# A recurrence of 64 chunks: corrections in two sets, new orders on four engines, TensorE's loop closed at another place

## The reference, cut to what matters

```python
def step(carry, inp):
    W1c, b1c = carry
    xq, xk, xv, et = inp
    Z1 = xk @ W1c + b1c
    grad = _ln_l2_bwd(Z1, xv - xk, g, bb)
    Attn1 = jnp.tril(xq @ xk.swapaxes(-1, -2))
    b1_bar = b1c - jnp.tril(et) @ grad
    Z1_bar = xq @ W1c - et * Attn1 @ grad + b1_bar
    last_eta = et[..., -1, :, None]
    W1n = W1c - (last_eta * xk).swapaxes(-1, -2) @ grad
    b1n = b1c - (last_eta * grad).sum(-2, keepdims=True)
    return ((W1n, b1n), xq + _ln(Z1_bar, g, bb, EPS_IN))
```

## Time and profile before

| | us |
|---|---|
| median of 3 runs | 583.49 (583.01 to 584.29) |
| the profiled execution | 581.06 |
| its span, first to last instruction | 579.2 |
| busy: PE, DVE, ACT, POOL | 483.9, 432.1, 346.2, 327.8 |
| mean granted clock of TensorE, share of full speed | 0.959 |

### The profile page before, as it was taken

The page is one execution under the profiler, slowest core; times in us unless marked ns, Lnnn a source line. Parts: engine busy times, 40 slices in busy tenths (PEclk is TensorE's granted clock), DMA queues, the critical chain, the costliest instruction groups (busy, mean ns, idle before and its releaser), DMA issues.

```text
span 579.2 us, 30352 instructions
## 1 busy us (share of the span) xinstructions
PE 483.9 (84%) x12556; PEld 313.8 (54%) x12556; DVE 432.1 (75%) x1526; ACT 346.2 (60%) x1166; POOL 327.8 (57%) x590
## 2 busy tenths in 40 slices
PE   0699889898558789888888888888887699998996
PEld 0344334443346577777777676666675244456563
DVE  4757788888746789888888888888885667676652
ACT  2344334322246788888888889988885487553321
POOL 1276888787734466666666655565763667330112
PEclk9999989899858999999999999999997899998998
DMA  8310111111101011111111000011010500000123
GB/s 338 123 24 14 37 37 36 38 36 36 39 9 32 22 37 28 33 32 33 33 28 37 1 1 1 19 36 37 19 37 4 171 1 2 1 2 1 74 75 145
DMA packets 15136, 24.74 MB, mean 43 GB/s; under 512 B 4228, under 2 KB 4968, under 8 KB 15080
## 3 DMA queue, kind: packets, MB, share of 16 engines
q1 hardware_dynamic: 15080, 24.10, 13.8%
HBM read 11.50 MB, written 4.19 MB: 27 GB/s over the span
## 4 chain that ended last, share of the span: by engine, by line
PE 25%; DVE 24%; ACT 12%; issue 8%; POOL 2%; POOLq 0%; ACTq 0%
PE PS L1167 6%; PE PS L924 4%; PE PS L1255 3%; PE PS L906 3%; ACT work L1556 3%; PE PS L361 2%; DVE work L1341 2%; DVE work L1336 2%; DVE work L1322 2%; DVE work L1300 2%; DVE work L1319 2%; DVE PS L1338 2%; DVE PS L1323 2%; DVE PS L1302 2%; DVE PS L1325 2%
## 5 line engine op out<-in xcount | busy, mean ns | idle before, releaser
L1167 PE MATMUL PS<-work 32*32 32x32 f32 x4064 | 59.6, 194 | 37.9 <-DVE work L1341 21.0
L1167 PEld LDWEIGHTS PS<-work 32*32 32x32 f32 x4064 | 53.8, 108 | 43.4 <-issue 43.1
L1411 POOL TENSOR_TENSOR work<-work,mask 128x256 f32<-128x256 f32 x64 | 46.8, 731 | 35.7 <-ACT work L1531 35.7
L512 PE MATMUL PS<-X,work 128*128 128x512 f32 x128 | 63.2, 641 | 0.3 <-ACT X L435 0.3
L1423 POOL TENSOR_TENSOR work<-work,lrh 128x4 f32<-128x4 f32 x64 | 12.9, 201 | 75.6 <-DVE work L1314 70.1
L1300 DVE TENSOR_REDUCE work<-work 128x4 f32<-128x128 f32 x64 | 18.3, 286 | 49.2 <-ACT work L1556 49.2
L663 POOL TENSOR_TENSOR work<-work 128x512 f32<-128x512 f32 x32 | 43.8, 1370 | 7.1 <-DVE work L582 7.1
L1152 PEld LDWEIGHTS PS<-work 64*32 64x32 f32 x2048 | 32.9, 110 | 24.9 <-issue 23.6
L1152 PE MATMUL PS<-work 64*32 64x64 f32 x2048 | 43.6, 225 | 2.9 <-issue 2.0
L1194 PE MATMUL PS<-cst 128*128 128x256 f32 x126 | 45.1, 440 | 0.0
L1179 PE MATMUL PS<-work 32*64 32x32 f32 x2016 | 43.0, 222 | 2.2 <-issue 2.2
(11 more groups left out here) (162 smaller groups left out, 1344.5 us busy)
## 6 DMA issues: line engine op xcount, KB each, us to landing
X<-in_x SPq DMA_DIRECT2D x4, 1024.0 KB, 8.2
TK<-KP SPq DMA_DIRECT2D x64, 64.0 KB, 1.9
X<-QP SPq DMA_DIRECT2D x64, 64.0 KB, 2.0
TK<-in_x SPq DMA_DIRECT2D x16, 256.0 KB, 3.0
out<-TK SPq DMA_DIRECT2D x16, 256.0 KB, 2.4
work<-in_rope SPq DMA_DIRECT2D x2, 512.0 KB, 9.1
cst<-in_consts SPq DMA_DIRECT2D x1, 289.0 KB, 5.0
work<-in_wk SPq DMA_DIRECT2D x1, 256.0 KB, 11.2
```

The source lines that it names most:

```text
L512: mm = nc.tensor.matmul(PS[:, 2 + m, :], lhs(j), xt(i, j), start=(j == 0), stop=(j == J - 1))
L1167: mm = nc.tensor.matmul(PS[HD * a:HD * a + HD, bank, b * width:b * width + HD], AM[p][HD * a:HD * a + HD, b, part, :, :].rearrange("p e t ...
L1411: nc.gpsimd.tensor_tensor(AM[p].rearrange("p b s e t -> p (b s) e t"), S1[p].unsqueeze(2).broadcast_to([P, 2 * B, E, CS]), mask2.rearrange ...
```

## The change

On VectorE the correction's two terms become operands of their own: WX moves from PSUM to SBUF, YC is made before cc1, one reduction and one product change places, and `out_var` comes ahead of GL. TensorE runs the correction twice, with YC as soon as that is there and with WX when that is (`front`), then waits for GL for the update and the attention. `front` holds corrections, update, attention and, where asked, the filler; `back` holds the next base and the query base. Chunks 0 to 1 and the front of 2 are written out, then come two loops, of 3 and of 12 trips, which begin with a back and end with a front, and then chunk 62's back and chunk 63. The filler is in the fronts 1 and 2 and in three of four fronts of the first loop.

VectorE's out_turn writes straight into TT; the tile ZT, ScalarE's `out_store` and the waits between them go, also those behind the last chunk (not shown: there `out_store` five times and four waits of VectorE). On GpSimd out_norm and queries come first; masks and blocks come last, behind a new wait for GL, in exchanged order. On ScalarE qt2 goes behind products.

```diff
...
@@ -754,11 +754,11 @@
         S1 = [carve(B * 2, CS) for _ in range(2)]
         AM = [carve(B, 2, E, CS) for _ in range(2)]
         Bs = [carve(B, HD) for _ in range(2)]
-        TS, SQ, YL, YC = (carve(B, HD) for _ in range(4))
+        TS, SQ, YL, YC, WX = (carve(B, HD) for _ in range(5))
         YY = carve(2, B, HD)
         GL = [carve(B, HD) for _ in range(2)]
         ZQ = [carve(B, HD) for _ in range(3)]
-        SQQ, ZN, ZT = (carve(B, HD) for _ in range(3))
+        SQQ, ZN = (carve(B, HD) for _ in range(2))
         ss, sz, ssq, sd1 = (carve(B) for _ in range(4))
         vq = [carve(2 * B) for _ in range(2)]
         var1, sdq = [v[:, 0:B] for v in vq], [v[:, B:2 * B] for v in vq]
...
@@ -1111,16 +1111,7 @@
 
                 return c >= n if isinstance(c, int) else n <= 2
 
-            def run_chunks(eng, body):
-
-                for c in range(2):
-                    body(c, c % 2)
-                with nc.Fori(0, NC // 4 - 1, engines=(mybir.EngineType.PE,), hint_back_edge=True) as four:
-                    for k in range(4):
-                        body(four * 4 + (2 + k), k % 2)
-                for c in range(NC - 2, NC):
-                    body(c, c % 2)
-
+            FILLED = 3
             GAIN_AT, PRE_AT = NC // 2 + 8, NC - 8
             QROWS_AT, PIECES, INPUTS_AT = 3, 2 * J * E, NC // 2 + 14
             is_last = lambda c: isinstance(c, int) and c == NC - 1
@@ -1160,14 +1151,14 @@
                         Bs[1 - p if past(n, 1) else 0], start=False, stop=False, skip_group_check=True
                         ).then_inc(q["base"], 1)
 
-                def grads(width, bank, p, part):
+                def grads(width, bank, p, part, rows):
 
                     for b in range(B):
                         for a in range(4):
                             mm = nc.tensor.matmul(PS[HD * a:HD * a + HD, bank, b * width:b * width + HD],
                                                   AM[p][HD * a:HD * a + HD, b, part, :, :].rearrange(
                                                       "p e t -> p (e t)"),
-                                                  GL[p][HD * a:HD * a + HD, b, :],
+                                                  rows[HD * a:HD * a + HD, b, :],
                                                   start=False, stop=True, skip_group_check=True)
                     return mm
 
...
@@ -1194,36 +1185,12 @@
                     nc.tensor.matmul(PS[:, QB[p], 256:512], ident, ccol("spread", 0, 256), start=True, stop=True,
                                      skip_group_check=True)
 
-                def body(c, p):
-
-                    o = 1 - p
-                    done, now, nxt = value(pe, c), value(pe, c + 1), value(pe, c + 2)
-                    before = value(pe, c - 1) if past(c, 2) else None
-                    if past(c, 1):
-                        pe.wait_ge(q["init"], 1)
-                        pe.wait_ge(q["gl"], done)
-                        pe.wait_ge(q["am"], done)
-                        pe.wait_ge(q["s1"], now)
-                        grads(ZW, ZB[p], o, 1).then_inc(q["corr"], 1)
-                        pe.wait_ge(q["init"], 1)
-                        pe.wait_ge(q["khx"], done)
-                        pe.wait_ge(q["bcopy"], done)
-                        update(o)
-                        grads(HD, QB[o], o, 0).then_inc(q["attn"], 1)
-                        if past(c, 2):
-                            pe.wait_ge(q["zq"], before)
-                        filler(p)
-                    else:
-                        base(0, 0, 1, 1)
-                    if not is_last(c):
-                        base(c + 1, o, nxt, now)
-                    else:
-                        pe_mean(pe, 0, True)
+                def query_base(ready, p, drained):
                     pe.wait_ge(q["init"], 1)
-                    pe.wait_ge(q["qt2"], now)
-                    pe.wait_ge(q["wcopy"], now)
-                    if past(c, 2):
-                        pe.wait_ge(q["zq"], before)
+                    pe.wait_ge(q["qt2"], ready)
+                    pe.wait_ge(q["wcopy"], ready)
+                    if drained is not None:
+                        pe.wait_ge(q["zq"], drained)
                     for b in range(B):
                         for k in range(J):
                             for a2 in range(2):
@@ -1231,14 +1198,59 @@
                                 mm = nc.tensor.matmul(
                                     PS[HD * a:HD * a + HD, QB[p], b * HD:b * HD + HD],
                                     QT2[p][r:r + 64, k * B + b, :, :].rearrange("p e t -> p (e t)"),
-                                    R[o][r:r + 64, k, b, 0:HD], start=(b == 0), stop=False,
+                                    R[1 - p][r:r + 64, k, b, 0:HD], start=(b == 0), stop=False,
                                     skip_group_check=True)
                     mm.then_inc(q["qbase"], 1)
 
-                run_chunks(pe, body)
+                def front(p, before, done, now, fill):
+
+                    o = 1 - p
+                    pe.wait_ge(q["init"], 1)
+                    pe.wait_ge(q["yc"], done)
+                    pe.wait_ge(q["am"], done)
+                    pe.wait_ge(q["s1"], now)
+                    grads(ZW, ZB[p], o, 1, YC)
+                    pe.wait_ge(q["init"], 1)
+                    pe.wait_ge(q["w"], done)
+                    grads(ZW, ZB[p], o, 1, WX).then_inc(q["corr"], 1)
+                    pe.wait_ge(q["init"], 1)
+                    pe.wait_ge(q["gl"], done)
+                    pe.wait_ge(q["khx"], done)
+                    pe.wait_ge(q["bcopy"], done)
+                    update(o)
+                    grads(HD, QB[o], o, 0, GL[o]).then_inc(q["attn"], 1)
+                    if fill:
+                        if before is not None:
+                            pe.wait_ge(q["zq"], before)
+                        filler(p)
+
+                def back(c, p, before, now, nxt):
+
+                    if not is_last(c):
+                        base(c + 1, 1 - p, nxt, now)
+                    else:
+                        pe_mean(pe, 0, True)
+                    query_base(now, p, before)
+
+                base(0, 0, 1, 1)
+                back(0, 0, None, 1, 2)
+                front(1, None, 1, 2, True)
+                back(1, 1, None, 2, 3)
+                front(0, 1, 2, 3, True)
+
+                for first, trips, fill in ((2, FILLED, True), (2 + 4 * FILLED, NC // 4 - 1 - FILLED, False)):
+                    with nc.Fori(0, trips, engines=(mybir.EngineType.PE,), hint_back_edge=True) as four:
+                        for k in range(4):
+                            c, p = four * 4 + (first + k), k % 2
+                            before, done, now, nxt = (value(pe, c + n) for n in (-1, 0, 1, 2))
+                            back(c, p, before, now, nxt)
+                            front(1 - p, done, now, nxt, fill and k < 3)
+                back(NC - 2, 0, NC - 3, NC - 1, NC)
+                front(1, NC - 2, NC - 1, NC, False)
+                back(NC - 1, 1, NC - 2, NC, None)
                 pe.wait_ge(q["gl"], NC)
                 pe.wait_ge(q["am"], NC)
-                grads(HD, QB[1], 1, 0).then_inc(q["attn"], 1)
+                grads(HD, QB[1], 1, 0, GL[1]).then_inc(q["attn"], 1)
 
                 def project(i, first):
                     if has(i, 2):
...
@@ -1291,8 +1303,9 @@
                 def out_turn(c):
 
                     dve.wait_ge(q["zn"], c + 1)
-                    nc.vector.transpose(ZT.rearrange("p b d -> p (b d)"), ZN.rearrange("p b d -> p (b d)")
-                                        ).then_inc(q["zt"], 1)
+                    nc.vector.transpose(
+                        TT.rearrange("p e (b n) -> p b e n", b=B)[:, :, :, c * CS:(c + 1) * CS],
+                        ZN.rearrange("p b (e t) -> p b e t", e=E)).then_inc(q["ot"], 1)
 
                 def body(c, p):
                     zb = PS[:, ZB[p], 0:B * ZW].rearrange("p (b n) -> p b n", b=B)[:, :, 0:HD]
@@ -1319,29 +1332,29 @@
                     nc.vector.tensor_tensor(YY[:, 0, :, :], PZ, TS, ALU.add).then_inc(q["y"], 1)
                     dve.wait_ge(q["y"], c + 1)
                     dve.wait_ge(q["zc"], c + 1)
+                    nc.vector.tensor_reduce(sums[:, 0:B], YY[:, 0, :, :], AX.X, ALU.add).then_inc(q["my"], 1)
                     nc.vector.tensor_tensor(YY[:, 1, :, :], YY[:, 0, :, :], ZC, ALU.mult).then_inc(q["yp"], 1)
-                    nc.vector.tensor_reduce(sums[:, 0:B], YY[:, 0, :, :], AX.X, ALU.add).then_inc(q["my"], 1)
-                    dve.wait_ge(q["yp"], c + 1)
-                    nc.vector.tensor_reduce(sums[:, B:2 * B], YY[:, 1, :, :], AX.X, ALU.add).then_inc(q["m"], 1)
                     dve.wait_ge(q["u"], c + 1)
                     dve.wait_ge(q["my"], c + 1)
                     nc.vector.scalar_tensor_tensor(cc0, sums[:, 0:B], -1.0 / HD, lead[:, 0, :],
```

(37 more changed lines are left out.)

15 lines of the change are left out of this document (3 added, 12 removed).

## The result

The changed kernel takes **618.5 us** in the median of 4 runs (612.65 to 625.47), where the kernel before took 583.9 beside it: a ratio of 1.052, 95% interval 1.045 to 1.059. The ratios in this document leave out executions that are over 1.5% longer than the fastest of their kernel, as two of these four are; the medians, and the profile shown here, do not. The forecast was slower, 596.8 and at most 613. Of the loss of 35 us, 13 were foreseen. The profiled execution is one of the two long ones, 623.56, with a granted clock of 0.863 in place of 0.959; a shorter one is under a0_again.

The account below looks back on a forecast made before the run. VectorE's chain into GL was taken to bound the recurrence's chunks. Terms 3.3 + 1.4 - 1.0 + 5 + 7.5 - 2.9 = +13.3 on the profiled 581.06 gave 594.4, and 2.43 for the median gave 596.8 us; range 586 to 613.

Parts of the forecast that it names:

- Period b + 2.86, S1 last: Recurrence: a chunk lasts 2.86 us beyond b, the base's first load, with S1 last; 4.11 unfilled, 4.28 filled.
- the 4.56 of the edge: Chunk at TensorE's loop closing, now behind the attention: base starts at +1.70 instead of 1.25, 4.56 us unfilled.
- GpSimd's second say: GpSimd's out_norm, queries, masks, blocks end at +5.43 and hold back the base two chunks on; period 4.30 us.
- Gain chunks: The 8 chunks with a gain on ScalarE: 35.6 us against 36.68, -1.0, without the two qt2 ahead of products.
- The end: Chunks 62 and 63: the code break comes only behind base(63), 10.6 us against 13.48, -2.9.
- First trip's code: Up to the first trip's end: 192 more loads, 1.54 blocks, 5.9 us, some falling into waits: +5.
- Second loop's code: Second loop's first trip: 808 new loads, 6.46 blocks, 24.9 us against 17.1: +7.5, bounds 4 and 10.
- The clock without filler: Rival: TensorE's clock falls to half without filler, 44 chunks by 1.7, some 670 us; chance 0.06.
- not kept: Rival: first loop's code is fetched again, 612 us, chance 0.12; the second loop's too, about 700, 0.04.
- code unnoticed: Rival: code arrives while TensorE waits for others, so the code terms fall away: 587.2 us; chance 0.04.
- second set alone: Faster rival: the second correction set, from WX, alone decides the recurrence's period, 3.74: 576 us; chance 0.08.

Follow-up runs that it names:

- a0_again: The changed kernel once more with no edit, beside other experiments: 619.8 us, ratio 1.055 to the kernel before.
- x8: The kernel before with TensorE's loop closing behind the attention, one loop, filler in all four chunks of a trip: 580.4 us, ratio 0.994.
- x12: The changed kernel with one loop of 15 trips and filler in all four chunks of each: 594.3 us, ratio 1.014.
- x2: The changed kernel with one loop of 15 trips in place of two, filler in three of four chunks: 595.1 us, ratio 1.020.
- x1: The changed kernel with filler in three of four chunks of the second loop too: 610.3 us, ratio 1.045.
- x14: The kernel before with one loop closing behind the attention, all four chunks filled, output transposed straight into TT, qt2 behind products: 578.8 us, ratio 0.988.
- x10: The changed kernel with one loop, all four chunks filled, one correction from GL, GpSimd's old order without its GL wait: 585.1 us, ratio 1.000.
- x4: The changed kernel with one loop, three of four chunks filled, GpSimd's order of before and no wait for GL there: 594.0 us, ratio 1.016.
- x5: The changed kernel with one loop, three of four chunks filled, one correction from GL in place of two: 613.2 us, ratio 1.051.
- x13: The kernel before with TensorE's loop closing behind the attention, cut into loops of 3 and 12 trips, all chunks filled: 588.4 us, ratio 1.005.
- x9: The kernel before without its filler and the wait ahead of it: 595.6 us, ratio 1.021.
- x7: The kernel before with TensorE's loop closing behind the attention, one loop, filler in three of four chunks: 595.7 us, ratio 1.017.

## Why the prediction was wrong in size

The runs make a ladder from before to after: closing behind the attention 583.9 to 580.4 (x8), **-3.5**; the recurrence to 594.3 (x12), **+13.9**; the fourth filler out to 595.1 (x2), +0.8; the loop cut in two to 610.3 (x1), **+15.2**; no filler in the second loop to 619.8, **+9.5**. By the ratios, which take out what chips differ by, the steps are -3.6, +11.6, +3.4, +14.9 and +5.8, each uncertain by 1 to 5; the third can't be told from nothing.

x14 and x10 divide the recurrence's 11.6: the direct output and ScalarE's order -3.2 (x8 to x14), VectorE's order with WX in SBUF +6.6 (x14 to x10), the second set with GpSimd's order +8.2 (x10 to x12). Steady trips of 16.4, 16.7 and 17.4 agree. So neither the second set nor VectorE's new order was worth having.

*Period b + 2.86, S1 last*: right. S1 is last, the loads follow the products by 0.48 (0.47 taken), and the periods alternate, 4.15 and 4.47 (4.11 and 4.30 taken). An unfilled trip is 17.25 (17.08), one with three fillers 17.28 in x2 (17.40). The base at +1.34 lies in the range given; the 4.56 of the edge doesn't show, its chunk is 4.47 as the one two on.

*GpSimd's second say*: right as a chain, and the wait for GL costs nothing in it. That the wait moves masks and blocks from GL (0.83 in x4 without it) to TS (0.62 in x5 with it) I didn't see.

*Gain chunks* -1.0: 36.0 in after and 35.9 in x2, where 35.6 was forecast. *The end* -2.9: x2 has 34.0 for chunks 56 to 63, 1.4 less than before, and x8 3.6 less. In after, at clock 0.59, it is 5.8 more. The term was right in its place and still bought nothing: chunks 61 and 62 take 10.4 in x2 (10.6 forecast, 13.5 before), but what lies behind the start of chunk 63 takes 2.9 more than before in x2 and 4.0 more in x8. The sum didn't look there.

*First trip's code* +5: too small. Chunks 0 to 8 take 8.0 more in x2 and 11.8 more in after; x8 without the second set 1.8 more. *Second loop's code* +7.5 (its own terms, 24.9 less 17.1, make 7.8), with bounds 4 and 10: 8.0 for the old recurrence (x13), 15.2 for the new one. The packets were counted rightly, and 7.3 us more without a load in x1's chunks 14 to 20 are near what it priced. The step that failed is the price of the chunks around them: I took each at full clock, and in these the clock is 0.55 to 0.76; in x1 the same loads take 6.5 longer for it.

*The clock without filler*: here the prediction broke. It compared busy shares, 80% and 79%, and from the gain chunks that keep 1.00 it gave the clock's fall 0.06, all or nothing, 44 chunks by 1.7. The 1.00 of the gain chunks was the filler's: x9 has 0.64 there. And the fall comes in part: 89 us of unfilled chunks run at full clock from 294.5 to 383.3, while two stretches of 44 and 41 us run at half, which begin at a wait for code and at a wait for GpSimd, in a0_again as well. In the sum the filler's leaving counted as a gain of 9 x 0.32 = 2.9 (17.40 to 17.08); it is a loss of 9.5 (5.8 by the ratios). With 12.4 there and 7.7 in the second loop's code, 20.1 of the missing 21.7 is found (by the ratios 8.7 and 7.4 of some 17). Of the 12.4, 2.6 are that an unfilled trip is hardly shorter (17.25 against 17.28); most of the rest is one term that the sum didn't have: the clock. For the change with one loop and filler the same steps give 583.5 + 12 x 0.69 - 1.0 + 5 - 2.9 = 592.9; x2 measured 595.1, near it in part by luck, as the first trip was priced too low, and so was what lies behind chunk 63, and the steady trip too high.

*The rivals*: "not kept" fell with 31 packets, "code unnoticed" with the breaks, "second set alone" with S1.

What stays open: which property of the filler keeps the clock, and why x7 loses it in some trips and not in others, behind waits that are as long in all of them. Nor is it shown why what lies behind chunk 63 is longer with the new closing. The rows give the places and the lengths, not the rule.

The Trainium skill (TensorE: Matmul & The Clock Gate, HAM oscillation — how this bites in real kernels) tells of a clock that is lost in waits between bursts of matmuls; x7 and x8 agree in kind, with a wait of 1.02 and one of 0.65; but x7 keeps its clock in other trips with the same wait.

## What to carry to other kernels

A matmul that computes nothing can be worth 13 to 15 us of 580: before it is taken out, or a wait is added to TensorE, look at the granted clock by stretch, and ask which work would bring it back. A second copy of a loop on TensorE has to pay for its code's arrival at the clock that the waits leave. A chain that is shortened on one engine needs the ring through all engines added up: here S1's ring of 4.23 lay just above GL's, 4.06 with VectorE's old order and 4.16 with the new one.

## What the hardware showed unasked

VectorE's operations with both operands in SBUF are longer beside GpSimd. The group of TS in after and in before:

```profile
L1321 DVE TENSOR_TENSOR work<-TK,work x64: 284/352/715, 169.9 to 486.2; 128x128 f32<-128x128 f32 x64
```
```profile
L1308 DVE TENSOR_TENSOR work<-TK,work x64: 285/286/423, 169.6 to 448.1; 128x128 f32<-128x128 f32 x64
```

In the chunk shown of after it took 0.63 and ended at 326.67, 0.15 behind blocks (325.91 + 0.61); in x5 0.15 behind blocks, and GL in x4 0.15 behind masks. The Trainium skill (SBUF — State Buffer, Who interferes with whom) says that a DVE instruction with two SBUF inputs contends with a GpSimd instruction that reads SBUF; these rows agree. The change moves WX from PSUM to SBUF, which makes GL such an instruction, and its wait on GpSimd keeps masks and blocks off GL, at TS's cost.

Half clock, once there, lasted 44 us although the listed gaps between TensorE's loads made only 0.60 in a chunk of 5.54; with filler it lasted 13.6 and 10.2 us at the same place (x1).
